# Projecting V behind the first pair of second scores, and Q of batch 4 a stage earlier, in a cross-attention and FFN kernel

## What is computed

```python
h = layernorm(x)                                  # (8, 256, 512)
q = h @ Wq.T + bq;  k = ctx @ Wk.T + bk;  v = ctx @ Wv.T + bv
scores = einsum("bgrqd,bgkd->bgrqk", q, k) / sqrt(16)   # 8 groups x 4 heads
w = softmax(where(mask, -inf, scores))
x = x + (w @ v) @ Wo.T + bo
h = gelu(silu(bitlinear(layernorm(x), w1, b1)))   # bitlinear: rms norm, 8 bit, ternary weights
x = x + bitlinear(layer_norm(h, ln_g, ln_b), w2, b2)
```

## Time and profile before

| what | value |
|---|---|
| median of 3 runs | 582.51 us (580.14 to 583.58) |
| the profiled execution | 581.34 us, of which 579.3 us are the span of the trace |
| mean granted clock of TensorE | 0.964 |
| busy: PE, DVE, ACT, POOL | 520.6, 491.1, 351.4, 139.9 us |
| start of stage 0 to 7 (DVE begins to split the maxima) | 56.0, 106.3, 159.1, 223.1, 285.7, 348.3, 411.9, 474.7 us |

### The profile page before, as it was taken

How to read it: one execution, slowest core, us unless ns; L and a number is a source line. 1 busy time by engine, 2 the same in 40 slices (tenths; PEclk the granted TensorE clock), 3 DMA queues, 4 the chain that set the end, 5 groups by cost and what they waited for, 6 DMA issues and landing times.

```text
span 579.3 us, 9027 instructions
## 1 busy us (share of the span) xinstructions
PE 520.6 (90%) x3425; PEld 285.6 (49%) x3425; DVE 491.1 (85%) x730; ACT 351.4 (61%) x424; POOL 139.9 (24%) x106
## 2 busy tenths in 40 slices
PE   4978788999899999899999999999949999798796
PEld 3856335544564557445663566445514553243343
DVE  4689929789989788988999789978896889959996
ACT  2235470687848764785659573866368576876931
POOL 5103034003410621025200611211122105133130
PEclk9986899999899999999999999999969999988999
DMA  6888595887126712463137502571115411110002
GB/s 200 277 209 317 174 279 156 335 304 170 37 66 197 163 43 79 160 179 86 72 117 183 117 16 98 161 170 40 43 39 140 101 40 42 27 30 1 36 2 75
DMA packets 32994, 72.17 MB, mean 125 GB/s; under 512 B 7167, under 2 KB 14529, under 8 KB 29950
## 3 DMA queue, kind: packets, MB, share of 16 engines
q1 hardware_dynamic: 31286, 67.13, 39.6%
q0 software_dynamic: 576, 4.19, 1.8%
q10 hardware_dynamic: 1088, 0.24, 0.2%
HBM read 46.50 MB, written 20.61 MB: 116 GB/s over the span
## 4 chain that ended last, share of the span: by engine, by line
PE 54%; DVE 20%; issue 8%; DMA 7%; ACT 7%; POOL 2%; SPq 2%; ACTq 0%; DVEq 0%
PE FF L891 8%; PE FF L943 6%; DVE negm L1416 5%; PE S L773 5%; PE PV L813 5%; ACT PT L1136 5%; PE PV L830 4%; PE S L797 4%; PE FF L710 3%; DMA num<-o_raw 2%; PE PV L773 2%; PE FF L893 2%; DVE work L1565 2%; POOL st L510 2%; PE FF L905 2%
## 5 line engine op out<-in xcount | busy, mean ns | idle before, releaser
L1136 ACT ACTIVATE PT<-S 128x1024 f32<-128x1024 f32 x128 | 123.4, 1032 | 24.0 <-PE S L797 23.6
L1416 DVE TENSOR_REDUCE negm<-S 128x4 f32<-128x1024 f32 x88 | 105.6, 1215 | 17.9 <-PE S L773 16.5
L797 PE MATMUL S<-Q,K 100*128 100x512 bf16 x256 | 73.7, 393 | 18.6 <-ACT PT L1136 14.9
L891 PE MATMUL FF<-w1t,xqT 128*128 128x512 bf16 x256 | 68.4, 390 | 5.0 <-ACT wq_sb L1170 3.4
L813 PE MATMUL PV<-PT,vaug 128*32 128x256 f32 x1024 | 70.5, 394 | 0.6 <-ACT PT L1136 0.6
L773 PE MATMUL S<-K,Q 97*128 97x256 bf16 x352 | 55.5, 284 | 5.4 <-DVE negm L1416 3.5
L830 PE MATMUL PV<-wo_sb,num 128*128 128x512 f32 x128 | 59.1, 608 | 0.0
L1170 ACT ACTIVATE work<-FF,s 128x512 f32<-128x512 f32 x48 | 33.0, 687 | 36.3 <-PE FF L893 36.3
L1416 DVE TENSOR_REDUCE negm<-PV 128x4 f32<-128x1024 f32 x40 | 48.8, 1220 | 5.6 <-PE PV L773 5.2
L710 PE MATMUL FF<-xnT,wq_sb 128*128 128x256 f32 x224 | 50.6, 381 | 0.2 <-ACT xnT L1103 0.2
L1194 ACT ACTIVATE work<-work 128x2048 bf16<-128x2048 f32 x12 | 22.9, 1911 | 45.2 <-DVE work L1571 45.0
(11 more groups left out here) (231 smaller groups left out, 905.2 us busy)
## 6 DMA issues: line engine op xcount, KB each, us to landing
Q<-q_d SPq DMA_DIRECT2D x15, 768.0 KB
q_d<-part SPq DMA_DIRECT2D x8, 768.0 KB, 3.6
x_sb<-in_x SPq DMA_DIRECT2D x8, 512.0 KB, 4.1
ctx_sb<-in_ctxT SPq DMA_DIRECT2D x8, 512.0 KB, 4.6
work<-in_w SPq DMA_DIRECT2D x4, 1024.0 KB, 13.2
q_d<-part SPq DMA_DIRECT2D x8, 512.0 KB, 3.3
xb_sb<-in_x SPq DMA_DIRECT2D x8, 512.0 KB, 4.3
work<-in_w POOLq DMA_DIRECT2D x4, 1024.0 KB, 8.9
```

The costliest lines, as they stand in the source:

```text
L797: last = pe.matmul(where, K[0:ROWS_2, g, kt * P:(kt + 1) * P], Q[0:ROWS_2, g, 2 * pair:2 * pair + 2, :], start=not masked, stop=True)
L891: pe.matmul(FF[:, n % 2, :], xqT[:, k, t * P:(t + 1) * P], w1t[:, k, cols], start=(k == 0), stop=False)
L1136: act.activation(PT[:, n % PT_SLOTS, :, :], ST[n % 2][:], ACT.Exp, scale=0.25).then_inc(S["pt_made"], 1)
L1416: dve.tensor_reduce(negm[:, t, R * g:R * g + R], RING_1[n % 3][:], AX.X, ALU.max, negate=True).then_inc(S["max_made"], 1)
```

## The change

Five things are moved, and one is added.

1. V of batches 2 to 7: `project_v(a)` no longer stands behind `project_k(a)` but behind the first pair of second scores; on ACT `values_in(a)` no longer stands ahead of the exponentials but behind the third.
2. V of batches 0 and 1: out of the start, into the first scores of batch 0 (behind numbers 2 and 4), written to FF; the context of batch 1 is loaded into `xb_sb`, so that it needn't wait for V of batch 0.
3. The transposed x and Q of batch 4: out of stage 2, into the first scores 10 to 15 of stage 1; on ACT the copy and the biases of that Q stand around the two Gelus of stage 1.
4. DVE in stage 2: `query_rests(4)` stands ahead of `spread_3` and the first `gain`, where it stood behind the second `shift`.
5. New: 11 matmuls of a tile of ones ahead of the first projection, once `ones` is set.

```diff
+        ctx_first = xb_sb[:].rearrange("p t n -> p (t n)").rearrange("p (k t) -> p k t", k=KD)
+        def ctx_of(a):
+            return ctx_first if a == 1 else ctx_sb[:, :, :]
+        def v_place(a):
+            return FFw[:, 512 * a:512 * a + 256] if a < 2 else FFw[:, 512:768]
         def x_front(a):
-            return S1[:, :, :] if a > 3 else front_of(a)
+            return S1[:, :, :] if a > 4 else front_of(a)
...
             def load_residual(c):
+                if at_start(c):
+                    sp.wait_ge(S["kv_ps"], 2)
...
# PE, turn_x(a)
-                if a > 3:
+                if a == 4:
+                    pe.wait_ge(S["silu_made"], 8)
+                if a > 4:
                     pe.wait_ge(S["max_made"], 16 * (a - 2) + 14)
...
# PE, body_of
-                w = next_front(a) if c > 1 else None
+                w = next_front(a) if c > 2 else None
...
                     project_k(a)
-                    project_v(a)
                 for g in range(G + 1):
                     if c is not None and g < G:
                         scores_2(c, 2 * g, masked)
                         scores_2(c, 2 * g + 1, masked)
+                    if g == 0 and a is not None and a > 1:
+                        project_v(a)
...
+                    if at_start(f):
+                        if n == 10:
+                            turn_x(4)
+                        if n >= 12:
+                            project_q(4, (n - 12,))
...
# PE, start
                     scores_1(0, n, masked)
+                    if n in (2, 4):
+                        project_v(n // 2 - 1)
...
+            pe.wait_ge(S["c_ones"], 1)
+            for _ in range(11):
+                pe.matmul(PV[:, 0, 0:P], ones[:], ones[:], start=True, stop=True)
             project_k(0)
             turn_x(0)
-            project_v(0)
...
             project_k(1)
-            project_v(1)
...
# ACT
-                    weight_abs_sum(0, (0, 1, 2))
+                    weight_abs_sum(0, (0,))
+                    values_in(0)
+                    values_in(1)
+                    weight_abs_sum(0, (1, 2))
...
                         exps(c, n)
+                        if n == 2 and a is not None and a > 1:
+                            values_in(a)
...
+                    if at_start(f):
+                        turned_x(4)
                     gelu(f, 0)
+                    if at_start(f):
+                        queries(4, 0)
                     gelu(f, 1)
                     deviations(f, 0)
+                    if at_start(f):
+                        queries(4, 1)
                     deviations(f, 1)
...
# DVE, body
-                if t is not None:
+                if t is not None and not at_start(t):
                     spread_3(t)
                     gain(t, 0)
...
-                if at_start(f):
+                if at_start(f) or at_start(t):
                     query_rests(w)
+                if at_start(t):
+                    spread_3(t)
+                    gain(t, 0)
```

More of the change, by code:

```diff
@@ L201, in front_flat @@
             return S0[:, :, :].rearrange("p r t -> p (r t)") if w == 1 else FFw
+        ctx_first = xb_sb[:].rearrange("p t n -> p (t n)").rearrange("p (k t) -> p k t", k=KD)
[3 more added lines that the diff above has]
+            return FFw[:, 512 * a:512 * a + 256] if a < 2 else FFw[:, 512:768]
         def x_front(a):
-            return S1[:, :, :] if a > 3 else front_of(a)
+            return S1[:, :, :] if a > 4 else front_of(a)
         def x_front_flat(a):
-            return S1[:, :, :].rearrange("p r t -> p (r t)") if a > 3 else front_flat(a)
+            return S1[:, :, :].rearrange("p r t -> p (r t)") if a > 4 else front_flat(a)
         def pair_of(a):
@@ L287, in load_context @@
             def load_context(a):
-                wait_for(sp, S["kv_ps"], a)
-                sp.dma_start(ctx_sb[:], ctxT[a]).then_inc(S["ctx_in"], 16)
+                if a > 1:
+                    sp.wait_ge(S["kv_ps"], a)
+                sp.dma_start(ctx_of(a), ctxT[a]).then_inc(S["ctx_in"], 16)
             def load_residual(c):
+                if at_start(c):
+                    sp.wait_ge(S["kv_ps"], 2)
                 wait_for(sp, S["x1_made"], 2 * c)
@@ L685, in turn_x @@
                 pe.wait_ge(S["xn_made"], 2 * a + 2)
-                if a > 3:
+                if a == 4:
+                    pe.wait_ge(S["silu_made"], 8)
+                if a > 4:
                     pe.wait_ge(S["max_made"], 16 * (a - 2) + 14)
                 if a == 2:
-                    pe.wait_ge(S["q_made"], 4)
-                    pe.wait_ge(S["r1q_made"], 4)
+                    pe.wait_ge(S["v_placed"], 2)
                 if a == 3:
@@ L721, in project_k @@
                     pe.wait_ge(S["r1k_made"], 1)
-                    pe.wait_ge(S["v_placed"], 1)
                 elif 1 < a < B - 1:
@@ L730, in project_k @@
                 for k in range(KD):
-                    last = pe.matmul(to[:, 0:T], wkv_sb[:, k, 0:P], ctx_sb[:, k, :],
+                    last = pe.matmul(to[:, 0:T], wkv_sb[:, k, 0:P], ctx_of(a)[:, k, :],
                                      start=(k == 0), stop=(k == KD - 1))
@@ L735, in project_v @@
             def project_v(a):
-                if a == 1:
-                    pe.wait_ge(S["v_placed"], 1)
-                to = pair_of(a)
+                if a == 0:
+                    pe.wait_ge(S["q_made"], 4)
+                    pe.wait_ge(S["r1q_made"], 4)
+                to = v_place(a)
                 for t in range(TT):
                     for k in range(KD):
-                        last = pe.matmul(to[:, 512 + t * P:512 + (t + 1) * P],
-                                         ctx_sb[:, k, t * P:(t + 1) * P], wkv_sb[:, k, P:2 * P],
+                        last = pe.matmul(to[:, t * P:(t + 1) * P],
+                                         ctx_of(a)[:, k, t * P:(t + 1) * P], wkv_sb[:, k, P:2 * P],
                                          start=(k == 0), stop=(k == KD - 1))
@@ L755, in scores_1 @@
                     pe.wait_ge(S["r1k_made"], 2)
-                    pe.wait_ge(S["v_placed"], 2)
                 if n == (0 if a > 0 else 4):
@@ L1128, in values_in @@
                 act.copy(vaug[:, a % 2, :, :, 0:HD],
-                         pair_of(a)[:, 512:512 + TT * P].rearrange("p (t g d) -> p t g d", t=TT, g=G)
+                         v_place(a).rearrange("p (t g d) -> p t g d", t=TT, g=G)
                          ).then_inc(S["v_placed"], 1)
@@ L1239, in body @@
                     turned_x(0)
-                    values_in(0)
                     queries(0, 0)
@@ L1251, in body @@
                     return
-                w = next_front(a) if c != 1 else None
+                w = next_front(a) if c not in (1, 2) else None
                 if w is not None and c > 0:
@@ L1266, in body @@
                     keys(a)
-                    values_in(a)
                 if c is not None:
@@ L1787, in body @@
                     quantise_weight(0, w1t[:].rearrange("p k n -> p (k n)"))
-                if w is not None and not at_start(f):
+                if w is not None and not at_start(f) and not at_start(t):
                     query_rests(w)
```

## The result

The changed kernel takes 587.0 us (median of 20 runs, 581.77 to 591.63) against 582.5 (20 runs) on the same chip, a ratio of 1.0065 with a 95% interval of 1.0039 to 1.009: slower by 0.65%. One of the 20, 591.63, counts as slow and is left out of the ratio; the others reach 590.05. Its profiled execution took 581.77, with a span of 579.8 against 579.3.

The account below looks back on a forecast made before the run. PE carries over half the chain, sharing second scores with ACT; stage heads belong to DVE and ACT. V -3.25, start -2.4 and stages 1 and 2 +7.1 sum to +1.5, giving 583.4; 8 in 10 from 577.5 to 588.

Parts of the forecast that it names:

- the prediction's own line of 585.4: Measured time above which it put the slower rival and part of the start's, 0.23; 0.5% (2.9 us) counts as telling.
- the forecast itself: Whole kernel: the main case, a time of 580.5 to 585, given 0.50.
- The mechanism of stage 2: Stage 2: split of Q and POOL's power delay DVE's second shift; exponentials start at 183.6 against 178.53, +5.0.
- The wait of 0.40: Stage 3: ACT's idling for PE until 245.28 goes, as the fourth exponential ends at 244.25; 1.0 us per stage.
- the price of the stall: Stage 5: DVE stalled beside POOL's add, so V gives 0; were the add elsewhere, the stage would give its 1.0.
- the forecast's case: Start: clock up when weights land, K ends at 9.8 and Q starts at 12.0 instead of 14.43, -2.4.
- the price of K's lower clock: Start: Q starts at 12.0 with the clock up (-2.4), 13.9 with it low (-0.5); the chain to the first maximum follows.
- the two V's between first scores: Start: V of batches 0 and 1 fall where DVE's maxima leave PE over half its time; cost 0.
- The second rival: Start doesn't move: clock not up, or Q's way through memory bound by bandwidth; +1.9 to +2.4 more, 585.5; chance 0.15.
- The first rival: Stage 2: PE alone releases the exponentials, -7.3 in all, 575; or half way, 578.5; together 0.22.
- the third (slower): Stage 2: clock stays down past the transposed FFN input, values 6 and 7 at half speed; 3 to 5 us, 587.5; 0.13.

Follow-up runs that it names:

- V alone: Kernel before with only V of batches 2 to 7 and its copy on ACT moved: 577.83 against 582.65, ratio 0.9917.
- third trace: Profile of the unchanged changed kernel, run again on one chip with its form with filled idle time: 588.17 against 583.19, ratio 1.0078; span 580.7.
- the start alone: Kernel before with V of batches 0 and 1 between first scores, batch 1's context elsewhere, 11 matmuls of ones: 581.02 against 582.65, ratio 0.9982.
- the whole: The changed kernel with all its parts against the kernel before: 587.0 against 582.5, then 589.65 against 582.65 and 588.17 against 583.19.
- Q alone: Kernel before with only Q of batch 4 moved into stage 1 and DVE's new order in stage 2: 590.39 against 582.65, ratio 1.013.
- first trace: First profiled execution of the changed kernel, 581.77, span 579.8; the kernel's median there was 587.0 against 582.5, ratio 1.0065.
- the filling: Changed kernel plus 90 unused matmuls in PE's idle time of stage 2: 583.28 against 583.47, ratio 1.0; again 584.69, ratio 1.0025.
- second trace: Profile of the unchanged changed kernel, run again on the chip of its three parts: 589.65 against 582.65, ratio 1.0122; span 587.2.

## Why the prediction was right or wrong

The forecast was 583.4, and the range of 8 in 10 ran from 577.5 to 588; the medians say 587.0 against 582.5, inside the range. They lie above the prediction's own line of 585.4, though, in the part to which it gave 0.23, and above the 580.5 to 585 that it gave to the forecast itself; on one of the other chips the kernel took 589.65. The mechanism of stage 2 was forecast, with its sign. The sum was made for an execution like the profiled one, where it gave +1.5 and the trace shows +0.5, and it said nothing of how executions differ. That these two are so close is in part luck, as the last paragraph shows.

**V behind the first pair.** Forecast -1.0 in stages 1, 3 and 4; measured -0.95 (V alone), -1.17 and -1.19. The wait of 0.40 went as worked out. Stage 6 gave 0.60 and not 0.25. Stage 5 was to give 0 because of POOL's addition. The first half of that holds: PE's wait grew by all that PE had gained (2.12 here). What the step left out is the clock behind the longer wait. Of eight profiled executions with V moved and the addition where it was, the wait is 1.99 to 2.18 in all, and stage 5 takes 63.6 to 63.7 in three and 65.0 to 65.1 in five. With the addition moved it is 61.6: 2.0 less than before the change, and up to 3.5 less than with V alone, where the prediction put the price of the stall at V's 1.0. By the Trainium skill (SBUF — State Buffer, section Who interferes with whom) DVE and GpSimd share a port pair as an exclusive lock, and a DVE instruction with at most one SBUF input outside the two-port modes doesn't contend. The traces agree in this: the stalled instruction was L1535, L1498 or L1631, whichever fell beside the addition, and the PSUM-fed L1652 kept its 1.29. Which mode an instruction was in, no run here shows.

**The start.** Forecast: Q at 12.0 if the clock is up when the weights land, 13.9 if not, and the whole chain moves by it. Q began at 13.40 in the first profiled execution, 13.82 and 12.20 in the other two. The third shows the forecast's case:
```profile
7.84 2.00 PE L742 MATMUL S<-ctx_sb,wkv_sb 128*128 128x256 f32 x8 [1.70 <-DMA wkv_sb<-in_wkv]
...
12.20 7.14 PE L722 MATMUL FF<-xnT,wq_sb 128*128 128x256 f32 x32 [1.19 <-ACT xnT L1123]
...
32.10 0.60 PE L784 MATMUL S<-K,Q 97*128 97x256 bf16 x4 [1.71 <-DMA K<-neg_d]
...
33.85 3.32 PE L753 MATMUL FF<-wkv_sb,ctx_sb 128*128 128x128 f32 x16
...
83.98 1.05 PE L784 MATMUL S<-K,Q 97*128 97x256 bf16 x8 [1.98 <-DMA K<-neg_d]
```
So the price of K's lower clock was right (the first maximum came at 33.54 instead of 35.70, -2.2), but three steps failed.

First, the good case was taken as the usual one. The ones end at 5.2 to 6.1 and the weights land at 7.8 to 8.3. In eight profiled executions with 11 of them K took 1.99, 1.99 and 2.00 behind waits of 1.68 to 1.75, 2.56 behind 1.90, and 3.40 to 3.68 behind waits of 2.33 to 2.90. Stage 0 then began at 54.5 to 54.8 in the first four and at 56.2 to 56.6 in the others; in the four profiled executions with the old start it began at 55.6 to 57.4. With 20 ones K took 1.99 and 1.98 in the two that were profiled.

Second, the two V's between first scores, priced at 0, cost something. From the first maximum to the beginning of stage 0 the old start took 20.3 in all four executions, the new one 20.9 to 21.3 in eight of ten. In the third trace V of batch 0 ran at the lower clock (3.32), and DVE then waited 0.89 for the first scores behind it.

Third, what the start gains gets lost behind stage 0's beginning, which the sum did not look at. In stage 0 the first scores wait for rows of K out of memory, which follow the stage's beginning: they landed 29.1 behind it before (85.03) and 29.2 in the third trace (83.98), so most of the 1.2 was still there. But PE waited 1.98 instead of 1.21 for them, and from there to stage 1 it took 23.4 instead of 21.3. That loss isn't the start's doing. With V alone, whose start is the old one, the same place shows
```profile
83.98 1.89 PE L773 MATMUL S<-K,Q 97*128 97x256 bf16 x8 [2.90 <-DMA K<-neg_d]
```
where the kernel before had 1.05 behind 1.21, and 24.6 to stage 1. The clock doesn't follow the wait alone: the rows took 1.89 behind 2.90, 2.08 and 4.48, and 1.05 behind 1.98, 2.25 and 2.50. The second rival (the start doesn't move), given 0.15, named K's clock, which was down in half of the eight, and the bandwidth of Q's way, which is not what took the gain; the start alone, at 0.9982, measured no gain that can be told.

**Q of batch 4.** Forecast +7.1 in stages 1 and 2 without V's share. The three executions of the whole give 5.9, 7.0 and 5.7, once V's 0.95 is added back, and Q alone gave 6.6 by its stages. Step by step, in the first trace: the last maximum begins 1.7 later in its stage with Q alone (1.8 forecast); from the end of the copy of the maxima to the end of the second shift 178.08 - 163.93 = 14.15 (14.25 forecast); from there to the exponentials 3.81 (3.8 forecast); from the first exponential to the transposed FFN input 13.3, and 14.0 and 13.2 in the other two traces (14.1 forecast). Stage 2 as a whole was to be about 6 longer and is 4.0 to 4.9. The first rival (PE sets stage 2) is excluded by the 10.79 of idle time. In the third (slower), values 6 and 7 were to run at half speed; they took 1.07 in all three traces, so it did not happen in that form.

**The sum.** In the profiled execution its terms were off in both directions: V gave -3.8 (with stage 1's 0.95 from V alone) for -3.25, the start and stage 0 -0.3 for -2.4, Q 5.9 for 7.1, and the end, for which it had no term, -1.25. That they add up to +0.5 beside +1.5 is luck as much as mechanism, the more so as stage 0 of the kernel before was profiled with a clock that three other executions of the same code didn't have. What the sum lacks against the medians, 584.0 against 587.0, goes with the granted clock: over 34 executions of the changed kernel the median granted clock is 0.956, over 66 of the kernel before 0.964. The 19 executions of the changed kernel at 0.956 or below took 589.2 in the median, the 10 at 0.961 or above 584.1; the profiled one had 0.964. At half speed the granted clock is 0.5, so a difference of 0.008 is 0.008 x 580 / 0.5 = 9 us more of it. Stage 2 alone has most of that: its granted clock was 0.98 before and is 0.93, 0.90 and 0.92 in the three traces, 7 to 11 us more of the lower level. The second trace shows more of it in stage 5 and at the end. The link is a reading of clocks and times side by side; the one run made to test it, the filling, showed 1.2 to 2.0 us in stage 2 and 3.5 in the median. What decides in one execution whether the clock falls is not shown; the same kernel did both.

## What to carry to other kernels

Before summing parts of a change, ask for each which engine comes last once the others are in: V's gain in stage 2 was real alone (1.2 of the stage's 2.16) and nothing beside Q's move. An instruction moved to give an idle engine work also moves what consumes its result; price that queue, here DVE's, in which 3.65 of split and a power on POOL stood in front of the shifts. And take a profiled execution's granted clock and place in the list of runs before you argue from it: a wait of 2 us on PE cost anything from nothing to 1.5 us behind it. The same holds for the kernel before: one profile of it had a stage 0 that was 1 to 3 us shorter than that of three other versions with the same code there.

## What the runs showed of the hardware

- DVE instructions of 128 x 2 to 128 x 6 elements took 2.12 to 2.36 instead of 0.2 beside a POOL addition of 128 x 1024 in SBUF, and 4.59 instead of 2.48 for two of 128 x 2048; a DVE instruction that read PSUM was not slowed.
- One kernel's K at the same place took 2.00, 2.56 or 3.45 in three executions, behind waits of 1.70, 1.90 and 2.90 us that followed 11 matmuls of ones; with PE busy until 7.3 or 8.2 it took 1.99 and 1.98.
- Rows of K of 2 KB landed 9.5 us after their issue in stage 0 of the third trace (74.44 to 83.93), behind 768 KB and 192 KB issued just ahead, and 10.6 in the version with idle time filled at two more places (75.50 to 86.09).
- Matmuls whose result nobody uses kept the granted clock at 1.00 through 14 us of stage 2, of which 11 otherwise showed 0.53, and slowed neither DVE nor ACT beside them (2.35 for a shift, 1.91 for the squares, with and without).
